# Carrying the lower experts' results with their rows, so that each row of out is added to once

## What is computed

```python
x = x + xattn(layernorm(x), ctx_1024, ctx_1024)          # scores * d**-0.5, causal, softmax
xt = layernorm(x).reshape(-1, 128)
logits = xt @ gate_w.T                                    # 8 experts
_, idx = top_k(logits + beta, 2)
probs = sigmoid(take_along_axis(logits, idx, axis=-1))
c = zeros((B, 8)).at[arange(B)[:, None], idx].add(probs)
g = einsum('bh,ehm->bem', xt, gate_proj_w); u = einsum('bh,ehm->bem', xt, up_proj_w)
eo = einsum('bem,emh->beh', silu(g) * u, down_proj_w)     # m = 256
combined = einsum('beh,be->bh', eo, c)
out = x + combined + shared_expert(xt)
```

## Time and profile before

| | us |
|---|---|
| median of 3 runs | 427.84 |
| lowest, highest | 426.01, 429.95 |
| the profiled execution | 426.79 |
| its span | 425.1 |

### The profile page before, as it was taken

How to read it: one execution, slowest core, us unless ns; L and a number is a source line. 1 busy time by engine, 2 the same in 40 slices (tenths; PEclk the granted TensorE clock), 3 DMA queues, 4 the chain that set the end, 5 groups by cost and what they waited for, 6 DMA issues and landing times.

```text
span 425.1 us, 10724 instructions
## 1 busy us (share of the span) xinstructions
PE 368.5 (87%) x3165; PEld 304.6 (72%) x3165; DVE 258.6 (61%) x1114; ACT 242.3 (57%) x575; POOL 288.7 (68%) x319
## 2 busy tenths in 40 slices
PE   8887999999989968899970999999999999999600
PEld 3444766665566545589970999999999999999600
DVE  5777999897788577666540455556555556556300
ACT  3696979887778564156550455655656555655200
POOL 7758788786658757305540358888888388888883
PEclk9999999999989999999995899999999999999955
DMA  6964336873222112155653467777555255554432
GB/s 211 367 191 156 120 132 214 241 233 124 94 95 83 57 52 70 58 140 90 95 89 89 90 102 120 115 111 116 75 76 71 41 69 74 73 72 51 38 34 22
DMA packets 56296, 46.23 MB, mean 109 GB/s; under 512 B 6824, under 2 KB 45488, under 8 KB 56240
## 3 DMA queue, kind: packets, MB, share of 16 engines
q1 hardware_dynamic: 39360, 34.49, 29.1%
q0 software_dynamic: 16880, 11.05, 20.6%
HBM read 26.79 MB, written 22.48 MB: 116 GB/s over the span
## 4 chain that ended last, share of the span: by engine, by line
PE 53%; POOL 12%; issue 11%; SPq 8%; ACT 4%; another core or an unknown queue 3%; DVE 2%; DMA 2%; POOLq 1%; ACTq 0%; DVEq 0%
PE gu_pair L1673 24%; PE bank L1692 13%; SPq L386 4%; POOL out L569 4%; POOL sorted_rows L527 3%; POOL rstd L488 3%; PE bank L1592 3%; PE bank L1613 2%; PE bank L1650 2%; ACT rows L749 2%; PE bank L1601 2%; SPq L372 2%; PE gu_pair L1550 2%; SPq L355 1%
## 5 line engine op out<-in xcount | busy, mean ns | idle before, releaser
L569 POOL DMA_INDIRECT out<-t_out,tile_in x103 | 160.0, 1553 | 82.8 <-DVE t_out L1280 48.2
L1673 PE MATMUL gu_pair<-tile_T,W_slot 128*128 128x128 f32 x1120 | 137.8, 277 | 0.5 <-ACT tile_T L817 0.5
L1673 PEld LDWEIGHTS gu_pair<-tile_T,W_slot 128*128 128x128 f32 x1120 | 132.0, 194 | 0.7 <-issue 0.7
L1259 DVE SCALAR_TENSOR_TENSOR t_hid<-t_silu,gu_pair 128x512 f32<-128x512 f32 (+1 forms) x71 | 48.3, 680 | 80.1 <-ACT t_silu L838 42.7
L838 ACT ACTIVATE t_silu<-gu_pair 128x512 f32<-128x512 f32 (+1 forms) x71 | 41.9, 590 | 91.4 <-PE gu_pair L1673 84.9
L828 ACT ACTIVATE W_slot<-W 128x512 f32 x140 | 80.0, 621 | 8.9 <-issue 5.7
L527 POOL DMA_INDIRECT sorted_rows<-rows,slot x64 | 64.6, 1010 | 23.3 <-issue 21.0
L1692 PE MATMUL bank<-W_down,t_hid 128*128 x560 | 75.1, 277 | 0.0
L1692 PEld LDWEIGHTS bank<-W_down,t_hid 128*128 128x128 f32 x560 | 69.0, 194 | 0.2 <-issue 0.2
L1601 PE MATMUL bank<-xn_T,shared_gu 128*128 128x512 f32 x64 | 33.0, 609 | 1.5 <-ACT silu_g L813 1.4
L1613 PE MATMUL bank<-shared_dn,hid 128*128 128x128 f32 x256 | 33.0, 284 | 1.1 <-DVE hid L1115 1.1
(11 more groups left out here) (153 smaller groups left out, 466.6 us busy)
## 6 DMA issues: line engine op xcount, KB each, us to landing
tile_in<-sorted_rows SPq DMA_DIRECT2D x103, 65.5 KB
x_sb<-x SPq DMA_DIRECT2D x16, 256.0 KB, 4.2
c_T<-ctx_cols SPq DMA_DIRECT2D x16, 256.0 KB
c_sb<-ctx SPq DMA_DIRECT2D x16, 256.0 KB
out<-acc SPq DMA_DIRECT2D x16, 256.0 KB
sorted_rows<-sorted_rows SPq DMA_DIRECT2D x56, 65.5 KB
sorted_rows<-padding SPq DMA_DIRECT2D x1, 2096.0 KB, 14.0
out<-t_out,tile_in POOLq DMA_INDIRECT x103
```

The source lines that it names most:

```text
L569: e.indirect_dma_start(out_flat, bass.IndirectOffsetOnAxis(ap=tile_in[:, n % NR, ID:ID + 1].bitcast(I32), axis=0), t_out[:, n % NO], None, ...
L1259: e.scalar_tensor_tensor(out=t_hid[:, i % 2, 0:n * M], in0=t_silu[:, 0:n * M], scalar=0.5, in1=gate_up_pair[i % 2][1][:, 0:n * M], op0=ALU ...
L1673: r = e.matmul(bank[:, c:c + P], W_slot[:, i % TX, h, at:at + P], tile_T[:, i % TX, tile], start=True, stop=True, skip_group_check=True)
```

## The change

The rows of one pair now lie two rows apart (`STRIDE` = 2), and each pair has a lane of its own of 2 x 8192 rows (`LANE`). The free row behind each row takes the weighted result of the lower expert. `sorted_rows` grows to 128 + 62 x 8192 rows of 131 numbers. A tile with its free rows is `WIDE` = 262 numbers for each of 128 rows.

The items stand in this order: 15 full tiles, the 17 double slots of the lower experts, 14 full tiles, and the 17 double slots of the higher experts with the last 8 full tiles among them. So tiles 15 to 47 are the lower experts', 62 on the higher experts' and the last full ones.

Results of the lower experts are not added to `out`. SP stores them (`store_part`) into the free rows of their tiles; that of tile n stands ahead of the load of tile n + 15 (`BEHIND`). When the last one, tile 47, is stored and landed, SP issues the 28 copies of k = 1, now from the lower experts' lists into the higher experts' lists, rows and results together, in 16 pieces, and the paddings; then it loads the first tile of a higher expert with both halves. DVE adds the carried result when it weights the higher expert's. GpSimd makes 70 adds. The copies of a k are issued in a new order (`parts_in_turn`), four lists in turn. The padding lies in x_sb, which is free by then, and is cleared by GpSimd behind the last scatter. Only the first 128 rows of each lane are filled at the start, in place of 4096 rows.

```diff
-    order = [(0, p) for p in range(HEAD)]
-    for k in (1, 2):
-        among = (FULL - HEAD - TAIL) // 2
-        for d in range(DUALS):
-            order.append((k, d))
-            if (d + 1) * among // DUALS > d * among // DUALS:
-                order.append((0, sum(kind == 0 for kind, _ in order)))
...
+    HEAD, MID = 15, 14
+    lowers, highers = [(1, d) for d in range(DUALS)], [(2, d) for d in range(DUALS)]
+    wholes = [(0, p) for p in range(FULL)]
+    order = wholes[:HEAD] + lowers + wholes[HEAD:HEAD + MID]
+    last = wholes[HEAD + MID:]
+    for d in range(DUALS):
+        order.append(highers[d])
+        order += last[d * len(last) // DUALS:(d + 1) * len(last) // DUALS]
...
-    parts = [[(r, l) for r in range(LISTS) for l in range(LISTS) if r < parts_of(k, l)] for k in range(2)]
+        def parts_in_turn(k):
+            longest = sorted(range(LISTS), key=lambda l: -parts_of(k, l))
+            turn = [[(r, l) for r in range(parts_of(k, l))] for l in longest]
+            ways = LISTS // 2 + 1
+            run = turn[:ways]
+            for later, first in zip(turn[ways:], reversed(run)):
+                first.extend(later)
+            return [run[w][r] for r in range(LISTS) for w in range(ways)]
+        partial = [n for n in range(TILES) if order[slot_with[n]][0] == 1]
+        NI, NS = 12, 4
...
+            def rows_of(at, pieces=P):
+                return sorted_rows[bass.DynSlice(at, STEP), :].rearrange("(p c) w -> p (c w)", p=pieces)
...
+                w = WIDE if kind == 2 else ROW
+                e.dma_start(tile_in[:, n % NR, 0:w], rows_of(rows_at[n])[:, 0:w]).then_inc(s_t_in[n % NI], 16)
+            def store_part(n):
+                s = partial.index(n)
+                e.wait_ge(s_t_out, n + 1)
+                if s >= NS:
+                    wait_done(e, partial[s - NS])
+                e.dma_start(rows_of(rows_at[n])[:, ROW:WIDE], t_out[:, n % NO]).then_inc(s_part_out[s % NS], 16)
...
+            def find_parts(k, r, l):
+                some = [m for m in (range(l, LISTS // 2 + 1) if l <= LISTS // 2 else range(l, LISTS)) if r < parts_of(k, m)]
+                to = row_numbers(part_row[0:1, k, r, l:l + len(some)])
...
-                e.dma_start(sorted_rows[bass.DynSlice(part_at[k, r, l], P, STRIDE), :],
-                            sorted_rows[bass.DynSlice(P + part_of(k, r, l), P, STRIDE), :]).then_inc(s_listed[l], 16)
+                if k == 0:
+                    e.dma_start(rows_of(part_at[k, r, l])[:, 0:ROW], rows_of(P + part_of(k, r, l) * LANE)[:, 0:ROW]
+                                ).then_inc(s_listed[l], 16)
+                else:
+                    e.dma_start(rows_of(part_at[k, r, l], 16), rows_of(part_at[0, l - r, r], 16)).then_inc(s_listed[l], 16)
...
             for n in range(TILES):
+                while stored < len(partial) and partial[stored] + BEHIND <= n:
+                    store_part(partial[stored])
+                    stored += 1
+                    if stored == len(partial):
+                        for m in partial[-NS:]:
+                            wait_done(e, m)
+                        fill_lists(1)
...
-                if n >= HEAD:
-                    fill_lists(1, 1)
...
             for n in range(TILES):
-                add_to_out(n)
-                if n in DRAINED:
+                if n not in partial:
+                    add_to_out(n)
+                if n == HEAD - 1:
                     e.drain()
...
+                            e.scalar_tensor_tensor(out=t_out[:, n % NO, 0:D], in0=y_h, scalar=weight, in1=tile_in[:, n % NR, ROW:ROW + D],
+                                                   op0=ALU.mult, op1=ALU.add).then_inc(s_t_out, 1)
```

More of the change, by code:

```diff
@@ L128, in build @@
         x_sb = sb("x_sb", [P, RX, GT, D])
+        padding = x_sb[:, :, :, :].rearrange("p r t d -> p (r t d)")[:, 0:PADS * WIDE].rearrange("p (n w) -> p n w", n=PADS)
         c_sb = sb("c_sb", [P, RC, GT, D])
@@ L249, in part_of, with wait_done @@
             return path.index((l, l + 1 + r) if k == 0 else (r, l + 1))
-        parts = [[(r, l) for r in range(LISTS) for l in range(LISTS) if r < parts_of(k, l)] for k in range(2)]
-        def added(n):
-            return 16 * (n // NR + 1)
+        def parts_in_turn(k):
[6 more added lines that the diff above has]
+            return [run[w][r] for r in range(LISTS) for w in range(ways)]
+        parts = [parts_in_turn(k) for k in range(2)]
+        assert all(sorted(parts[k]) == sorted((r, l) for l in range(LISTS) for r in range(parts_of(k, l))) for k in range(2))
+        def added(n):
+            return 16 * sum(m not in partial for m in range(n % NR, n + 1, NR))
+        def wait_done(e, n):
+            if n in partial:
+                s = partial.index(n)
+                e.wait_ge(s_part_out[s % NS], 16 * (s // NS + 1))
+            else:
+                e.wait_ge(s_t_added[n % NR], added(n))
+        NI, NS = 12, 4
+        partial = [n for n in range(TILES) if order[slot_with[n]][0] == 1]
         s_const, s_pairs, s_warm = sem("const"), sem("pairs"), sem("warm")
@@ L294, in build @@
         s_listed = [sem(f"listed{l}") for l in range(LISTS)]
-        s_t_in = [sem(f"t_in{i}") for i in range(NR)]
+        s_t_in = [sem(f"t_in{i}") for i in range(NI)]
         s_t_transposed, s_tile_T = sem("t_transposed"), sem("tile_T")
@@ L300, in build @@
         s_t_added = [sem(f"t_added{i}") for i in range(NR)]
-        CONSTS = 17
+        s_part_out = [sem(f"part_out{i}") for i in range(NS)]
+        CONSTS = 16
         PAIR_STEPS = 14
-        DRAINED = (HEAD - 1, 58)
+        BEHIND = 15
         def scatters(g):
@@ L561, in add_to_out @@
                     e.wait_ge(s_stored[1], 16 * G // 2)
-                if order[i] == (1, 0) and n == tiles[i][0]:
+                if order[i] == (2, 0) and n == tiles[i][0]:
                     for m in range(PADS):
-                        e.wait_ge(s_t_added[m], added(m))
-                if order[i] == (2, 0) and n == tiles[i][0]:
-                    last = max(m for m in range(n) if order[slot_with[m]][0] == 1)
-                    for m in range(last - NR + 1, last + 1):
-                        e.wait_ge(s_t_added[m % NR], added(m))
+                        wait_done(e, m)
                 e.indirect_dma_start(
                     out_flat, bass.IndirectOffsetOnAxis(ap=tile_in[:, n % NR, ID:ID + 1].bitcast(I32), axis=0),
-                    t_out[:, n % NO], None, compute_op=ALU.add
+                    t_out[:, n % NO, 0:D], None, compute_op=ALU.add
                 ).then_inc(s_t_added[n % NR], 16)
@@ L596, in padding_consts @@
             def padding_consts():
-                e.memset(padding[:, 0:FILL], 0.0).then_inc(s_const, 1)
+                e.memset(blank[:], 0.0).then_inc(s_const, 1)
                 e.wait_ge(s_const, 10)
@@ L609, in more_consts @@
                 e.memset(last_row[:], 0.0).then_inc(s_const, 1)
-                e.memset(padding[:, FILL:PADS], 0.0).then_inc(s_const, 1)
-                e.wait_ge(s_const, 16)
+                e.wait_ge(s_const, 15)
                 e.affine_select(out=last_row[:], in_=last_row[:], compare_op=ALU.not_equal, fill=1.0,
```

104 lines of the change are left out of this document (52 added, 52 removed).

## The result

The changed kernel takes 442.35 us (median of 4 runs, 438.08 to 445.97), the kernel before beside it 427.06 (4 runs, 426.01 to 429.95): a ratio of 1.031, 95% interval 1.022 to 1.041. Ratios leave out runs of a slower state (here 445.97 and, in the last experiment, 415.14), while medians have them in. It is slower by 15 us; 430 with a range of 417 to 437 was forecast. The profiled execution of the changed kernel took 442.76, its span is 440.7.

What follows compares the result with a forecast made beforehand. GpSimd's adds bound the end and SP's issue time the holes: TensorE resumes at 333.2, first higher result at 346.3, plus 81.8 gives a 428.1 span, 3.0 over 425.1; written as 430 us, range 417 to 437.

Steps and rivals of the forecast that it cites:

- the second hole: TensorE idle before the first tile of a higher expert, waiting for SP's chain: 320.4 to 333.2, 12.8 us.
- A: The sum itself: SP's issue-bound copies leave a hole of about 13 us; 430 us, own range 425 to 435, chance 0.43.
- the new chain on SP: On SP after the last lower result: store, 28 copies (32.3 us), seven paddings (5.5), tile loads; TensorE resumes at 333.2.
- rival B: On SP, copies are issued quicker, at 0.15 us an issue: hole of 4 us, time 421, chance 0.29.
- rival D: On SP, short register loads cost what long ones do, 6.7 us more: slower, 437, chance 0.08.
- SP runs up to 15 tiles ahead: On SP, stores of 33 partial results, 0.33 to 0.43 us each, fit beside tile loads and cost nothing.
- the first hole: TensorE idle before the first list tile, waiting for SP's copies and paddings: 7.7 us instead of 12.5.
- The end: GpSimd is last: 41 adds 1.857 us apart, the span ending 81.8 us after the first higher expert's add.
- The closing piece: From the last add's start on GpSimd to the span's end: 7.5 us of landing and closing.
- Rival C: Copies of one list land late and hold up the next: hole 22.5 us, time 440, chance 0.12.
- rival E: The first stage is slower by some 5 us through the new spread of rows: 435, chance 0.08.

Runs made afterwards that it cites:

- the last experiment: Changed kernel with 18 full tiles ahead of the lower experts, 19 behind, fewer register loads, tile loads among copies, six other paddings later: 410.45 us, ratio 0.989.
- after again: The changed kernel, unchanged, profiled a second time: 425.48 us in one run, 1.027 times as long as the kernel before.
- the 128-piece kernel: The changed kernel with its copies of k = 1 in 128 pieces of 1048 bytes instead of 16 of 8384: 427.32 us beside 414.81.
- the experiment on them: The changed kernel with the six other paddings issued behind the fourth list tile's load instead of ahead of the first: 250.1 us from first sorted matmul to end.
- the kernel with fewer loads: The changed kernel with 10 loads of row numbers among the 28 copies of k = 1 instead of 28: 419.68 us, ratio 1.012.

## Why the prediction was wrong

From the first sorted matmul on, piece by piece (us):

| piece | forecast | after | after again |
|---|---|---|---|
| to the matmuls of item 44 | 133.4 | 136.2 | 133.9 |
| from there to those of item 45, the second hole in it | 16.8 | 23.5 | 22.2 |
| to the first higher expert's add | 10.9 | 11.0 | 11.0 |
| 40 steps to the last add | 74.3 | 74.3 | 74.3 |
| to the span's end | 7.5 | 8.4 | 8.3 |
| sum | 242.9 | 253.3 | 249.8 |

The kernel before has 239.9 and 240.2. So the forecast's +3 was +13.4 in the one pair of profiles and +9.6 in the other; the pair of the forecast adds 2.2 us of a longer first stage, not shown to be the change's. The mechanism was the right one, that of the forecast itself (A): two holes set by SP's issue, passed on to the end by the adds that follow. The step that failed is **the new chain on SP**, whose length was mis-sized:

| step of the chain (us) | forecast | after | after again |
|---|---|---|---|
| result of tile 47 to the issue of its store | 0.1 | 1.7 | 0.8 |
| to the first copy | 2.3 | 2.8 | 2.7 |
| 28 copies | 31.9 | 35.4 | 35.4 |
| seven paddings, to the end of issue | 5.4 | 5.8 | 5.9 |
| to the first tile load | 1.7 | 2.5 | 2.3 |
| to TensorE's start | 2.8 | 3.0 | 2.8 |
| less what TensorE has to do meanwhile | 31.4 | 31.8 | 31.8 |
| hole | 12.8 | 19.4 | 18.1 |

- **The issue of a copy, taken as 0.40 for being in fewer pieces, is 0.52** (28 x 0.12 = 3.4 us, all of the copies' miss). That was the upper bound, and the earlier trace rows had it: a copy of before is DRAM to DRAM, with a median of 0.52. The nearest row was the same kind of transfer, not the tile load. That pieces don't matter is shown with the 128-piece kernel; it also takes away the ground of rival B, which had the largest chance beside A.
- **The register loads were right**: 28 loads, 269 ns the shortest, 465 the median, 13.0 us in all as forecast; together with 0.52 for the issue the model gives the 35.4. (The forecast's 4.4 for nine loads and 4.8 for seven are not the 0.52 and 0.71 of the earlier trace rows, which make it 13.3 in all.) The Trainium skill, DMA: Bandwidth & Descriptors, section Latency and other measured facts, has a floor of some 0.6 us for them; the 0.27 here does not agree, and rival D falls with it.
- **"SP runs up to 15 tiles ahead" costed the stores at nothing, and was wrong for the last one.** The store of tile 47 stands behind a tile load and the store of 46; at the end of this stretch a pair of store and load takes 1.16 us, and in the first profile a long issue of 1.38 us at 292.88 made the last store 1.7 late. This is 0.7 to 1.6 us.
- **Landings were taken from one row of an easy case.** The earlier trace rows are paddings of 67 KB, 1.8 us; those of now are 134 KB each and, six in a row behind seven, land after 3.5 to 3.8 (3.2 to 3.9 in the repeat):

```profile
L501 SPq DMA_DIRECT2D sorted_rows<-x_sb x6: 431/446/461, 227.4 to 229.8; - x6
...
DMA to landing us min/median/max: 3.5/3.6/3.8
```

  From the end of their issue to the first list tile's load are 3.2 us (3.3 in the repeat), where 1.6 was forecast: this is 1.6 to 1.7 us of the first hole (10.5 and 9.3 against 7.7). In the repeat half of it was given back, as the clock was up again sooner (items 14 and 15 are 3.2 apart, not the 4.0 forecast). The 1.2 us between the two profiles are the k = 0 copies, which took 27.3 in the first and 26.1 in the repeat. Issued elsewhere the paddings land sooner, as the experiment on them shows; that it is what stands ahead of them and not their size alone is shown by that difference (2.9 against 3.8 at most), while how the rest divides stays open. The Trainium skill, same page and section, says that the fixed cost of a DMA is smaller when the memory is less loaded. The difference here goes that way, but no run tells the load of the memory from the place in the queue.
- **The end.** 41 adds 1.86 apart were right. The closing piece is 8.1 to 8.4 in all seven profiles with the change and 7.5 in both without; why was not tried, and its cause stays open.
- **Rival C** is refuted by the waits above and by the kernel with fewer loads, **rival E** is not borne out by the repeats.
- **The range.** Its top, 437, came from the rivals. The sum's own terms, each at its upper end, were not added up: with 0.52 for the issue alone the sum is 433.4, and five small terms (the late store, two landings, the closing piece, the paddings) all went the same way: whatever is left out of a serial chain can only make it longer. What the first table shows to be missing, 6.9 to 10.4 us, puts A at 437 to 440, where its own range ended at 435.

And the tell-tales: holes were promised at 223 to 231 and 320 to 333, and came at 226 to 236 and 326 to 345; copies 1.15 apart from 291 on came 1.26 apart from 298 on; the first of the last 41 adds, promised near 346, came at 358.

## What to carry to other kernels

A serial chain that begins only when the last result of a stage is there is paid in full, less the independent work kept for that moment: count the issues on its queue (copies, register loads, padding, landing at both ends), and size the independent work to it before moving anything else. Here 14 full tiles were kept and the hole was 18 to 19 us; with 19 kept, 18 ahead of the first chain, five tile loads among the copies, and 10 register loads instead of 28 the same idea is 1.1% faster than the kernel it started from, whose own hole was left as it is. For an operation that no row shows, take the duration of the same kind of transfer in the same queue, and give the range the sum of all the upper ends.

## What the runs showed of the hardware that was not expected

- On SP's queue the issue of a DMA from DRAM to DRAM takes 0.52 us, in 16 or in 128 pieces, with one or two addresses from registers; a tile load into SBUF takes 0.33 and a store of a result from it 0.36. Bytes don't set it either: a padding of 134 KB, from SBUF to DRAM as the store is, takes 0.33 at a row from a register (median, L438) and 0.45 at a fixed row (L501). What makes the fixed one dearer was not tried.
- Now and then a single issue takes 0.4 to 1.2 us more than the others of its kind. In the changed kernel's stretch of stores these are four, 13 us apart, of which one hit the last stores:

```profile
253.89 1.50 SPq L383 DMA_DIRECT2D tile_in<-sorted_rows  x1
...
267.04 1.33 SPq L383 DMA_DIRECT2D tile_in<-sorted_rows  x1
...
279.83 0.78 SPq L383 DMA_DIRECT2D tile_in<-sorted_rows  x1
```

  and the one at 292.88 above. What causes them is open.
- One and the same kernel took 12 us less for its first stage in its second profile (173.0 against 185.2), and the same within 0.3 us in the rest (240.2 against 239.9). Whether the chip or something else makes the difference is open; stages are safer to compare than spans.
